# First quad's stacks written part by part from SBUF, tasks behind the first units, shift stores begun on ScalarE, new placement tables

## The reference, cut to what matters

```
x: (2, 1024, 128) f32, 16 heads of width 8
xn  = layernorm(x)
Q,K = rope(xn @ wq.T), rope(xn @ wk.T);  V = xn @ wv.T
A   = softmax(causal(Q K^T / sqrt(8)))
out = x + (A V) @ wo.T + (xn @ CB.T) * (SCB / 127) + bias
```

## Time and profile before

| what | us |
|---|---|
| median of 3 runs (lowest, highest) | 259.69 (259.62, 261.62) |
| the profiled execution, device time | 259.88 |
| its span, first to last instruction | 258.2 |
| granted TensorE clock over the span | 0.980 of 2.4 GHz |

### The profile page before, as it was taken

The page is one execution under the profiler, slowest core; times in us unless marked ns, Lnnn a source line. Parts: engine busy times, 40 slices in busy tenths (PEclk is TensorE's granted clock), DMA queues, the critical chain, the costliest instruction groups (busy, mean ns, idle before and its releaser), DMA issues.

```text
span 258.2 us, 10150 instructions
## 1 busy us (share of the span) xinstructions
PE 240.1 (93%) x4294; PEld 124.1 (48%) x4294; DVE 218.7 (85%) x594; ACT 183.6 (71%) x360; POOL 103.6 (40%) x169
## 2 busy tenths in 40 slices
PE   6888896888999999999999999999999999999945
PEld 6546541233344555554554465445555554436334
DVE  7899268999999999989999998999889989962072
ACT  2045732273997888779788878889889799999701
POOL 7570724749856391293233032304401430440300
PEclk9999998699999999999999999999999999999997
DMA  7625758620230467162027103700770210010602
GB/s 196 220 66 150 202 120 156 144 46 4 67 85 23 106 165 129 44 165 67 5 81 165 29 4 103 158 18 3 192 163 5 90 41 4 3 44 20 182 10 84
DMA packets 23559, 22.96 MB, mean 89 GB/s; under 512 B 2757, under 2 KB 20549, under 8 KB 23513
## 3 DMA queue, kind: packets, MB, share of 16 engines
q1 hardware_dynamic: 23368, 22.05, 34.3%
q10 hardware_dynamic: 144, 0.26, 0.4%
HBM read 13.70 MB, written 8.39 MB: 86 GB/s over the span
## 4 chain that ended last, share of the span: by engine, by line
PE 72%; DVE 13%; ACT 5%; DMA 4%; SPq 2%; issue 2%; POOL 1%; ACTq 0%
PE psA L918 22%; PE psB L918 20%; PE psV L990 18%; DVE prod L802 8%; ACT ring L697 3%; PE psB L906 2%; PE psB L901 2%; PE psA L1030 2%; DMA qs<-shiftsT 2%; SPq L384 2%; DMA rest<-o_scratch 2%; PE psA L872 1%; DVE rest L815 1%; PE psB L872 1%; ACT xnT L639 1%
## 5 line engine op out<-in xcount | busy, mean ns | idle before, releaser
L802 DVE CUSTOM_DVE_ANT_0 prod<-psA,cmask 128x128 f32<-128x128 f32 (+7 forms) x256 | 177.9, 754 | 16.7 <-PE psA L918 15.6
L697 ACT ACTIVATE ring<-psB 128x512 f32<-128x512 f32 x288 | 154.5, 608 | 33.6 <-PE psB L918 30.7
L918 PE MATMUL psB<-qs,ks 128*32 128x512 bf16 (+3 forms) x1536 | 99.2, 327 | 0.5 <-DMA qs<-shiftsT 0.2
L918 PE MATMUL psA<-ks,qs 128*32 128x512 bf16 (+3 forms) x1536 | 94.7, 334 | 5.3 <-DVE mx L802 4.5
L990 PE MATMUL psV<-ring,va 128*32 128x512 f32 (+3 forms) x768 | 76.0, 486 | 0.1
L918 PEld LDWEIGHTS psB<-qs,ks 128*32 128x32 bf16 x1536 | 40.8, 96 | 48.6 <-ACT ring L697 24.2
L559 POOL TENSOR_SCALAR_AFFINE_SELECT ring<-ring 128x512 f32<-128x512 f32 x64 | 40.0, 642 | 48.2 <-ACT ring L697 48.2
L918 PEld LDWEIGHTS psA<-ks,qs 128*32 128x32 bf16 x1536 | 34.2, 96 | 43.8 <-DVE mx L802 28.0
L539 POOL CAST shifts<-mx 128x16 bf16<-128x16 f32 x16 | 3.2, 198 | 71.0 <-DVE mx L802 71.0
L990 PEld LDWEIGHTS psV<-ring,va 128*32 128x32 f32 x768 | 22.5, 110 | 16.6 <-issue 8.9
L802 DVE DVE_READ_ACCUMULATOR2_ANT mx<- 128x1 f32 x256 | 21.3, 83 | 0.0
(11 more groups left out here) (89 smaller groups left out, 157.0 us busy)
## 6 DMA issues: line engine op xcount, KB each, us to landing
qs<-q_scratch SPq DMA_DIRECT2D x48, 96.0 KB
ks<-k_scratch SPq DMA_DIRECT2D x48, 96.0 KB
o_scratch<-ot SPq DMA_DIRECT2D x12, 256.0 KB, 2.6
q_scratch<-ot SPq DMA_DIRECT2D x20, 128.0 KB, 2.5
k_scratch<-ot SPq DMA_DIRECT2D x12, 128.0 KB, 2.5
x_sb<-x SPq DMA_DIRECT2D x4, 256.0 KB, 4.5
rope_sb<-rope SPq DMA_DIRECT2D x2, 512.0 KB, 6.8
rot<-o_scratch SPq DMA_DIRECT2D x3, 256.0 KB, 3.5
```

What stands on the lines that cost most here:

```text
L697: act.activation(ring[:, s % P_RING, k * HALF:(k + 1) * HALF], bank_b(e % B_RING), ACT.Exp)\
L802: last = dve.tensor_tensor_reduce(masked_scores[:, u % 2, at:at + w], psA[:, (u % 2) * SEQ + at:(u % 2) * SEQ + at + w], cmask[:, SEQ - w: ...
L918: mm = pe.matmul(psum[strip:strip + STRIP, at:at + size], keys[:, strip:strip + STRIP], queries, start=True, stop=True)
```

## The change

Six things are changed.

1. The stacks of quad 0 no longer go through HBM. SP writes each part of 32 partitions (the first quad's channels) straight to the 8 rows of each of the 3 groups: 18 DMAs of 32 KB for each half, 36 in all, at the head of SP's queue. For this the channels of a quad lie by channel and then by head (`swap`, `rope_tables`, the scratch layout). The stores to HBM follow, and the loads for quad 1 behind them.
2. `FIRST_TASKS` goes from 5 to 2. The tasks for c = 4 and 5, "max", and those for batch 1 stand behind units 2 to 19 of quad 0. The turning of the last 512 rows (`turn_rows(3)`) moves behind unit 7.
3. All 22 units of quad 0 stand ahead of the first bank (13 before).
4. Rows 8 to 15 are normalised on ACT instead of DVE, the variance's epsilon is added on DVE instead of POOL, Q's and K's second remainders of the second round go from DVE to POOL, and each projection releases its product by itself.
5. Each shift store is begun by ACT, directly behind its copy, with a wait on that copy, and is no longer in SP's queue.
6. All tables by bank are new, and `PROJECT_BANK`, `TURN_FIRST`.

```diff
 UNIT_BANK = [
-    [AHEAD, AHEAD, AHEAD, AHEAD, AHEAD, AHEAD, AHEAD, AHEAD, AHEAD, AHEAD, AHEAD, AHEAD, AHEAD, 36, 36, 36, 37, 37, 37, 39, 41, 43],
-    [8, 8, 8, 9, 9, 9, 12, 14, 15, 16, 18, 20, 21, 23, 25, 27, 28, 29, 30, 31, 32, 33],
+    [AHEAD, AHEAD, AHEAD, AHEAD, AHEAD, AHEAD, AHEAD, AHEAD, AHEAD, AHEAD, AHEAD, AHEAD, AHEAD, AHEAD, AHEAD, AHEAD, AHEAD, AHEAD, AHEAD, AHEAD, AHEAD, AHEAD],
+    [2, 4, 5, 6, 8, 9, 12, 13, 15, 16, 18, 19, 21, 22, 24, 26, 28, 29, 30, 32, 33, 35],
...
-    [-7, -5, -4, -2, 0, 1, 2, 5, 5, 8, 10, 11, 13, 13, 16, 18, 20, 22, 24, 26, 29, 30],
+    [-5, -3, -1, 1, 2, 5, 5, 7, 9, 11, 11, 14, 15, 17, 18, 22, 22, 25, 26, 29, 31, 33],
 ]
 TURN_BANK = [
-    [AHEAD, 44],
+    [AHEAD, 40],
...
-    [14, 37],
+    [16, 39],
 ]
 VALUE_BANK = [
...
-    [11, 20, 22, 26, 29, 32, 35, 37, 37, 38],
+    [12, 15, 17, 21, 24, 27, 30, 37, 38, 38],
 ]
 SAVE_BANK = [
...
-    [23, 43],
+    [18, 52],
 ]
...
-PROJECT_BANK = [269, 276, 296]
-TURN_FIRST = 292
+PROJECT_BANK = [261, 271, 296]
+TURN_FIRST = 285
...
-TASKS = [("v", 0), ("ffn", 0), ("late", 4), ("late", 5), ("v", 1), ("ffn", 1), ("late", 6), ("late", 7),
-         ("max", 0)]
-FIRST_TASKS = 5
-
-TASK_AFTER = {(5, 0): 0, (5, 1): 1, (6, 0): 2, (6, 1): 2, (7, 0): 3, (7, 1): 3, (8, 0): 8}
+TASKS = [("v", 0), ("ffn", 0), ("late", 4), ("late", 5), ("max", 0), ("v", 1), ("ffn", 1), ("late", 6), ("late", 7)]
+FIRST_TASKS = 2
+
+TURN_AFTER = 7
+ROWS3_FIRST = 4
+TASK_AFTER = {(2, 0): 2, (2, 1): 2, (3, 0): 4, (3, 1): 4, (4, 0): 9, (5, 0): 9, (5, 1): 11, (6, 0): 12, (6, 1): 14, (7, 0): 15, (7, 1): 16, (8, 0): 18, (8, 1): 19}
...
+            def stack_part(c, n):
+
+                hf, stack = c // 2, (qs, ks)[c % 2]
+                if n < 2:
+                    sp.wait_ge((part1, part2)[n], c + 1)
+                else:
+                    sp.wait_ge(part3[c], 1)
+                for g in range(PARTS):
+                    row = g * GROUP + ((n - g) % PARTS if c % 2 == 0 else n) * DH
+                    sp.dma_start(stack[row:row + DH, 0, hf, :, :], part(c, n)[0:QUAD * DH, :]).then_inc(stack_in[0][hf], 16)
+
+            sp.wait_ge(pads0_ready, 2)
+            for n in range(PARTS):
+                for c in (0, 1):
+                    stack_part(c, n)
+            stack_part(2, 0)
+            stack_part(2, 1)
+            stack_part(3, 0)
+            stack_part(3, 1)
+            stack_part(2, 2)
+            stack_part(3, 2)
             store_parts(0)
-            sp.wait_ge(pads0_ready, 2)
+            store_parts(1)
+            sp.wait_ge(pads1_ready, 2)
             sp.wait_ge(scratch_out[0], 16 * ROUND_DMAS)
-            load_stack(0, 0)
-            store_parts(1)
+            load_stack(1, 0)
             sp.wait_ge(scratch_out[1], 16 * ROUND_DMAS)
-            load_stack(0, 1)
-            sp.wait_ge(pads1_ready, 2)
-            load_stack(1, 0)
             load_stack(1, 1)
-            store_shifts(0, 0)
             sp.wait_ge(pads2_ready, 2)
             load_stack(2, 0)
             load_stack(2, 1)
-            store_shifts(0, 1)
             for i in range(1, QUADS):
-                store_shifts(i, ORDER[i][0])
...
+            def normalise(g):
+                act.wait_ge(shift_ready, g - 1)
+                for t in range(4 * g, 4 * g + 4):
+                    act.activation(xn[:, t, :], x_sb[:, t, :], ACT.Identity, bias=mean_shift[:, t:t + 1],
+                                   scale=rstd[:, t:t + 1]).then_inc(xn_late_ready, 1)
...
                 act.activation(shiftsT[:, hf, :], bank_b(e % B_RING)[0:2 * 16, 0:P], ACT.Copy).then_inc(exp_done, 1)
+                act.wait_ge(exp_done, e + 1)
+                shift_rows = qs[SHIFT:SHIFT + NSHIFT, i % SLOTS, hf, :, :].rearrange("r h (t q) -> r (h t) q", q=P)
+                act.dma_start(shift_rows, shiftsT[:, hf, :]).then_inc(shift_in[hf], 16)
```

More of the change, by code:

```diff
@@ L384, in load_stack @@
                         sp.dma_start(stack[g * GROUP:(g + 1) * GROUP, slot, hf, :, :],
-                                     source[heads, first:first + PARTS, :, tok:tok + HALF]
-                                     .rearrange("h p d t -> (p d) h t")).then_inc(ready, 16)
+                                     source[i % 4, first:first + PARTS, :, :, tok:tok + HALF]
+                                     .rearrange("p d h t -> (p d) h t")).then_inc(ready, 16)
                 if i >= SLOTS:
@@ L439, in _ @@
                         store_heads(done, hf)
-                if i + 2 < QUADS:
+                if 1 < i and i + 2 < QUADS:
                     if i == 2:
@@ L604, in masks @@
                         copy_v(i, 1)
[L605 to L612, removed]
+                if i == 1 and 3 <= s < 7:
+                    add_ffn(s - 3)
+                if i == 2 and 3 <= s < 7:
+                    add_bias(s - 3)
+            beside(-3)
+            pads(qs, 2, 0.0, pads2_ready)
+            pads(ks, 2, TWO_MINUS_ONES, pads2_ready)
+            for n in (-2, -1):
                 beside(n)
@@ L666, in save_task @@
                 last.then_inc(task_saved, 1)
+            def normalise(g):
[3 more added lines that the diff above has]
+                                   scale=rstd[:, t:t + 1]).then_inc(xn_late_ready, 1)
             turned_rows(0)
+            parts_of(0, 0)
             turned_rows(1)
-            for n in range(2):
-                parts_of(0, n)
-                parts_of(1, n)
+            parts_of(1, 0)
+            parts_of(0, 1)
+            parts_of(1, 1)
+            normalise(2)
+            parts_of(2, 0)
             turned_rows(2)
+            parts_of(2, 1)
+            parts_of(3, 0)
             save_task(0)
+            parts_of(3, 1)
+            for n in range(1, ROWS3_FIRST):
+                save_task(n)
+            normalise(3)
             turned_rows(3)
[L676 to L680, removed]
-            for n in range(2, len(TASKS)):
+            for n in range(ROWS3_FIRST, len(TASKS)):
                 save_task(n)
@@ L703, in save @@
                 act.wait_ge(pv_done, i * NSTEPS + LAST[i][hf] + 1)
+                if i == 1 and hf == 0:
+                    act.wait_ge(part3[5], 1)
+                if i == 2 and hf == 0:
+                    act.wait_ge(xb_ready, 4)
                 act.activation(ot[:, i, hf * HALF:(hf + 1) * HALF], psV[:, :], ACT.Copy).then_inc(ot_saved, 1)
@@ L743, in statistics @@
                 last.then_inc(ln_step, 1)
+                dve.wait_ge(ln_step, 3 * g + 2)
+                bt = slice(4 * g, 4 * g + 4)
+                dve.tensor_scalar(var_eps[:, bt], mv[:, bt, 1], EPS, None, ALU.add).then_inc(ln_step, 1)
             def normalise(g):
@@ L781, in rotate, with third_part @@
                                   ALU.add).then_inc(rotated, 1)
-            rotate(0)
-            rotate(1)
+            def third_part(c):
+                dve.wait_ge(part2, c + 1)
+                dve.tensor_tensor(part(c, 2), rest[:, c % 2, :], part(c, 1), ALU.subtract).then_inc(part3[c], 1)
+            for c in (0, 1):
+                product(c, 0)
+                product(c, 1)
+                rotate(c)
             leave(0)
             leave(1)
-            normalise(2)
-            dve.wait_ge(part2, 2)
-            dve.tensor_tensor(part(1, 2), rest[:, 1, :], part(1, 1), ALU.subtract).then_inc(part3[1], 1)
-            normalise(3)
+            product(2, 0)
+            third_part(1)
+            product(2, 1)
             rotate(2)
+            product(3, 0)
+            product(3, 1)
             rotate(3)
-            leave(2)
-            leave(3)
+            statistics(3)
             def maximum(i, u):
@@ L1103, in rope_tables @@
     for ch in range(P):
[L1104 to L1106 removed]
+        d = ch % (QUAD * DH) // QUAD
+        table[ch, 0] = cos[:, d // 2]
+        table[ch, 1] = sin[:, d // 2] if d % 2 else -sin[:, d // 2]
     return table
```

134 lines of the change are left out of this document (77 added, 57 removed), and 24 rows, old and new, of tables (UNIT_BANK, VALUE_BANK).

## The result

| | before | after |
|---|---|---|
| median of the runs of this comparison, us (lowest, highest; 4 each) | 259.66 (259.62, 261.62) | 277.94 (276.73, 278.67) |
| span of the profiled execution, us | 258.2 | 274.9 |
| granted TensorE clock over the span | 0.980 | 0.957 |
| first bank's exponential, us | 47.69 | 60.32 |
| quad 1's first exponential | 80.6 | 95.65 |

The ratio is 1.068, 95% interval [1.062, 1.074]: 7% slower. The profiled execution took 276.73 us.

The account below looks back on a forecast made before the run. PE and DVE were taken to bound quads 0 and 1, PE quads 1 to 6, ACT and the chain the end. Terms -2.2 + 1.0 + 0.4 + 0.75 - 2.4 = -2.5 us from 259.88 gave 257.4 us, range 252 to 262.5.

Parts of the forecast that it names:

- Its stack is covered: Quad 1's stack: 16 stores and 12 loads put its first half in place at about 53.5 us, needed at 56.5.
- late loads for quad 1: Rival, SP's queue: 0.75 us an issue, 36 issues take 4 us more, stacks come later; 261 us, chance 0.07.
- The stack writes: SP's 36 issues, 0.64 us apart from 14.4 us: units 0 and 6 filled 3.6 and 1.9 us earlier.
- cheap issues would not help either: Direct writes: 8 rows get 54 GB/s, an estimated 0.60 us for 32 KB, so transfers are no faster than issues.
- The tasks: PE, units 6 to 21: 14.7 us plus 1.7 of mutual waiting with DVE; first bank filled at 55.5 us.
- slow clock: Rival: PE at half clock behind idle stretches; 3.4 us lost, 260.8 us, with two stretches 264; chance 0.20.
- Quad 0's banks: PE's new tables and DVE's work for quad 1: quad 1's first exponential at 78.4 us against 80.6, 2.2 us gained.
- Quads 1 to 6: PE's new tables leave 138.8 us of work there instead of 137.8: 1.0 us lost.
- Shift stores on ACT: ACT, 0.75 us each: 0.4 us charged from 80 to 205 us, bounds nothing to some 3; 0.75 lost in last quad.
- ACT as the bound: Rival: the stores' 0.75 us pass on to PE in quads 4 to 7; 3 us more, 260 to 261, chance 0.13.
- stack loads go out earlier: SP's queue without shift stores, quads 1 to 6: no row shows PE waiting for those loads, so valued at nothing.
- The end: Last quad: the first half's copy moves from bank 23 to 18, five exponentials of 0.49 us each; 2.4 us gained.

Follow-up runs that it names:

- f1: The changed kernel with only the first quad's 32 channels in the new order and the HBM copy by heads as before, complete computation: 267.14 us, 1.027.
- e1: The changed kernel with the HBM copy in the shape of before, stores and loads both; serves for time only: 266.95 us, 1.026 to before.
- e2: The changed kernel with only the stores to HBM in the shape of before, loads in the new one; time only: 265.84 us, 1.022 to before.
- f2: The changed kernel without direct writes: old layout, quad 0's stack through HBM; task order, tables and shift stores on ACT kept: 261.01 us, 1.003 to before.
- g1: The changed kernel without direct writes, old HBM copy, shift stores back in SP's queue; task order and new tables kept: 256.98 us, 0.989 to before.
- g3: The changed kernel with the HBM copy repaired, nine of the first half's eighteen writes (K's) begun by ACT: 267.04 us, 1.030 to before.
- f4: The kernel before with only the shift stores begun on ACT behind their copies: 272.02 us, 1.047.
- e3: The changed kernel with only the loads from HBM in the shape of before, stores in the new one; time only: 285.28 us, 1.097 to before.
- f6: The kernel before with only four numbers changed: last quad's first-half values at banks 12, 15, 17 and its copy at bank 18: 258.07 us, 0.9945.
- f5: The kernel before with only the last quad's rows of the tables and the change's `PROJECT_BANK` and `TURN_FIRST`: 260.10 us, 1.002.

## Why the prediction was wrong

Forecast 257.4 us, range 252 to 262.5; measured 277.94. In the profiled execution 19.3 us are missing: 17.3 by quad 1's first exponential (95.65 instead of 78.4), 3.6 in quads 1 to 6, and at the end 1.6 us were gained more than I said.

**The step that failed: "Its stack is covered".** I priced the change's 16 stores and 12 loads with the rows of before, and said that quad 1's first half would be in place at 53.5 us, "needed at 56.5 us; were it later, each us would be a us". It was in place at 68.9 us. The layout in HBM is part of the change, I had listed it, and gave it no price. It costs 277.94 - 267.14 = 10.8 us by f1, 11.0 by e1, 12.1 by e2, all of it in the stores, which run on 4 of the 16 DMA engines. The rival *late loads for quad 1* (0.07, 261 us) had the place and the consequence right; its cause, slow issues of the 36 writes, was not the main one, and its size, 4 us, was too small.

**The stack writes.** Right: they start at 14.35 us (14.4), and cost what reads SBUF costs; the pace was 0.70 us, 0.06 above my value. So the last write began at 39.2 us instead of 36.8, unit 6 at 41.5 instead of 39.1 us, unit 0 at 29.05 instead of 27.5. Wrong was the comparison "3.6 and 1.9 us earlier than before". Before, units 0 and 6 were filled at 31.08 and 40.98 us, but that was PE behind its tasks and DVE, not the stacks, as the prediction itself says; f2 shows what the way through HBM gives once the tasks are moved: 27.90 and 38.61 us. The change's real rival for the same place was its own task order without its direct writes, and the writes lose 1.2 and 2.9 us to it (0.7 and 3.9 by g1). With what follows, they cost 6.1 us. I worked out the direct way against the old kernel's fill times, not against the old way under the new order. Wrong too was "cheap issues would not help either": the transfers took 0.23 us and not 0.60 (g3). It did not enter the sum.

**The tasks.** "PE needs 14.7 us there ... I add 1.7 us": from unit 6 to the first bank PE took 18.3 us (41.52 to 59.86), 1.9 more. The rival *slow clock* (0.20) was right in mechanism: 0.50 granted from 39.4 to 46.2 us, from within the pause of 4.17 us, with the work behind it on the path. It gave 3.4 us. How much of the 1.9 us is the clock's shows g1, where it was 1.00 from unit 6 on: the same stretch took 17.1 us (37.57 to 54.64), so about 1.3 us are the clock's and 0.7 were missing in my sum. In all the clock fell three times, each time behind or during such a pause (5.75, 4.17, 8.22 us).

**Quad 0's banks.** "2.2 us gained" came out where nothing else was in the way: in g1 quad 1's first exponential is at 78.16 us, 0.2 us from my 78.4. That it is so near is partly luck: g1 is at its first bank at 54.64 us instead of 55.5, since its stack comes by HBM, and takes 0.6 us longer from there. But the gain needs neither direct writes nor ACT's stores. (20.2 us at 0.962 are 21.0 and not 20.9, which changes nothing.)

**Quads 1 to 6.** "1.0 us lost" to the tables: g1 has 144.8 us against 143.3, so 1.5.

**Shift stores on ACT.** "I charge 0.4 us; the bounds are nothing and ... some 3 us", and 0.75 in the last quad. Measured: 148.4 - 144.8 = 3.6 us in quads 1 to 6 and nothing in the last quad (31.1 and 31.2 us); in the medians 4.0 us. The rival *ACT as the bound* (0.13, 3 us more) had the size right and belonged in the forecast. Its place, quads 4 to 7, it had wrong for these tables: there f2 loses 0.3 us to g1, and 3.2 of the 3.6 in quads 1 and 3. With the old tables of f4 2.1 of 3.3 us do lie in quads 4 to 6. That ACT's 21.1 us of pauses did not cover the stores, 10 of 0.75 us, is measured; that they come too seldom for a ring of three banks is how I read it, and no run with a longer ring was made. In quad 3 of f2 part of the loss is not ACT's time but the store's late landing. This is a cost that I had not seen at all: "stack loads go out earlier; ... I give it nothing". A shift store that ACT begins while stack loads are under way starts to move up to 9.1 us later (e3; 1.4 in before and 1.3 in g1, by SP), which held PE 6.35 us in f4, 7.0 at once in e3 and 2.07 in the change.

**The end.** "2.4 us gained": f6 alone gives 2.2 us in the last stretch, and by its ratio's interval 0.6 to 2.2 us of the whole. With the change's other rows for the last quad it is 3.1 us (f5, g1). Right mechanism, right size.

The medians account for the whole: layout 10.8, direct writes 6.1, shift stores on ACT 4.0, and the rest of the change -3.3 (g1 against its own before, 260.3), together +17.6 of 277.94 - 259.66 = 18.3 us. The 0.7 us between them are the kernel before, which had another median beside each group. By the ratios, times 260 us, the four are 10.7, 6.2, 3.6 and -2.8 and add up to the whole 17.7. The parts were undone one behind the other, so what two of them cost together stands with the first: f1's wait of 1.89 us for a shift store on ACT is in the 6.1 us of the direct writes.

What stays open: why the loads from the new layout take 0.76 us to issue instead of 0.38 (it cost nothing here: e2, which has it, is 1.1 us faster than e1), and how much of f2's first 57 us, 1.9 us longer than g1's up to the first bank with the same DMAs, is chance between two executions (the stores of the second round landed 1.3 us later, and a second stretch at half clock followed).

## What to carry to other kernels

When a change alters the layout of a buffer in HBM, count the DMA engines of each store and load again before any row of the old kernel is used as its price: here 1.28 us a store instead of 0.60, on a queue that everything else stood in. Compare a new way to an input with the old way under the new order, not with the time at which the old kernel used it, which may have been set by something else. Moving a small DMA to another engine's queue gives up the place it had among the big ones (6.35 us at once in f4) and costs the engine its issue (both together 3.6 us over six quads in f2).

## What the hardware showed that I had not expected

- 128 KB stores that run on four DMA engines hold back the queue that issues them: 0.54 us for the first, 1.28 us and more for the later ones, 96 GB/s. In the old shape the median is 0.60 us, the longest 1.9.
- Loads of the same 96 KB cost 0.38 us of SP's time from a layout by heads and 0.76 us from one in which a head's rows lie next to each other; the longer issue cost no time (e1 against e2).
- A DMA begun by another engine does not pass what is under way: an 8 KB store from ACT, 1.25 us to issue in f4, had its first packet 6.75 us after its start and reached the bank after 9.7 us, with stack loads of 96 KB begun ahead of it by SP.
- DMA share while the direct writes run alone (25.7 to 32.5 us): 0.14, at 48 GB/s, one 32 KB write, moved in 0.23 us, for each issue of 0.70 us: the pace was the issuing queue's.
